# Attention's 416 steps written out with constant waits and addresses; gathers that take their indices straight from the sorted table and from src

## What is computed

```
h = relu(layernorm(x))
# layer 0: idx = both directions of the edge list
ngl, ngr = (h @ Wl.T), (h @ Wr.T)                  # 4 heads of 16
gl, gr = ngl[idx_src], ngr[idx_dst]
score  = (att * leaky_relu(gl + gr, 0.2)).sum(-1)
alpha  = softmax of score over the edges of one idx_src
out    = segment_sum(gr * alpha, idx_src)
x = x + gelu(concat([out, h]) @ W1.T + b1) @ W2.T + b2
# layer 1
h = relu(layernorm(x))
agg = segment_sum(h[src] + edge_attr, dst)
y = relu(agg @ W1 + b1) @ W2 + b2
x = x + batchnorm(y)
```

## Time and profile before

| | |
|---|---|
| median of 3 runs | 9004.02 us (8930.97 to 9032.82) |
| the profiled execution | 9012.64 us, span 9010.8 us |
| attention, from its first gather to its last | 1127.5 to about 6308 us |
| messages, first gather | 6676 us |
| granted clock of PE | 0.537 of full speed in the mean |

### The profile page before, as it was taken

One profiled execution on the slowest core, in us unless ns is written; L12 is line 12 of the kernel. 1 busy time (PEld: TensorE's weight loads), 2 busy tenths in 40 slices (PEclk: granted clock), 3 DMA queues, 4 the chain that ended last, 5 costly groups with the idle time before them and its releaser, 6 DMA issues. The chain is left out here.

```text
span 9010.8 us, 65938 instructions
## 1 busy us (share of the span) xinstructions
PE 2933.2 (33%) x13731; PEld 2480.9 (28%) x13731; DVE 5072.6 (56%) x7913; ACT 1027.4 (11%) x1576; POOL 5385.2 (60%) x4913
## 2 busy tenths in 40 slices
PE   1011122533544333354444334343341112121223
PEld 1011122423434333353333334343220111111112
DVE  9999922745756565575656556564832323333334
ACT  3001100101111111011111101010210101001101
POOL 0000066767777776777777776777036666667774
PEclk9975555555555555555555555555555555555555
DMA  1000022323433333343333333337311111111211
GB/s 30 0 0 0 9 73 65 104 74 85 107 92 93 90 87 85 83 109 91 86 90 88 87 87 91 87 95 71 69 38 44 47 45 48 44 46 46 48 44 31
DMA packets 530967, 588.05 MB, mean 65 GB/s; under 512 B 274126, under 2 KB 277326, under 8 KB 530466
## 3 DMA queue, kind: packets, MB, share of 16 engines
q1 hardware_dynamic: 370066, 421.03, 15.4%
q0 software_dynamic: 156672, 160.75, 11.6%
q10 hardware_dynamic: 3984, 3.89, 0.2%
HBM read 467.65 MB, written 117.55 MB: 65 GB/s over the span
## 5 line engine op out<-in xcount | busy, mean ns | idle before, releaser
L827 POOL DMA_INDIRECT rows<-gr_table,stage x3328 | 3799.1, 1142 | 2345.4 <-DVE stage L1009 1319.7
L882 PE MATMUL bank<-gl_step,hot_t 128*128 128x64 f32 x6720 | 1562.6, 412 | 2205.7 <-issue 1395.0
L882 PEld LDWEIGHTS bank<-gl_step,hot_t 128*128 128x128 f32 x6720 | 1503.1, 327 | 2335.4 <-issue 1660.5
L1337 POOL DMA_INDIRECT message<-h_table,edge_stage x1568 | 1565.3, 998 | 781.8 <-issue 663.3
L1030 DVE TENSOR_TENSOR fore<-bank,rows 128x512 f32<-128x512 f32 x416 | 283.7, 682 | 1472.0 <-remote 803.5
L1358 PE MATMUL bank<-edge_parts,edge_hot 128*128 128x192 bf16 x1568 | 286.4, 363 | 1789.1 <-DVE edge_parts L1428 1201.5
L889 PE MATMUL bank<-parts,hot_sum 128*128 128x204 bf16 x3328 | 681.5, 374 | 484.0 <-issue 403.1
L1358 PEld LDWEIGHTS bank<-edge_parts,edge_hot 128*128 128x128 bf16 x1568 | 202.7, 140 | 1872.7 <-DVE edge_parts L1428 1259.7
L889 PEld LDWEIGHTS bank<-parts,hot_sum 128*128 128x128 bf16 x3328 | 508.3, 159 | 587.1 <-issue 451.0
L967 ACT CAST parts<-terms 128x544 bf16<-128x544 f32 x416 | 268.5, 645 | 2978.7 <-DVE terms L1038 1804.0
L1053 DVE TENSOR_TENSOR hot_sum<-iota_row,place 128x1024 bf16<-128x1024 f32 x416 | 504.5, 1213 | 6.8 <-issue 6.7
(11 more groups left out here) (267 smaller groups left out, 4355.4 us busy)
## 6 DMA issues: line engine op xcount, KB each, us to landing
place_b<-place_rows SPq DMA_DIRECT2D x422, 256.0 KB
gr_rows<-rows SPq DMA_DIRECT2D x416, 256.0 KB
rows_again<-gr_rows SPq DMA_DIRECT2D x416, 256.0 KB
rows<-gr_table,stage POOLq DMA_INDIRECT x3328
edge<-in_edge_attr SPq DMA_DIRECT2D x97, 512.0 KB
gl_step<-gl_table SPq DMA_DIRECT2D x844, 32.0 KB
message<-h_table,edge_stage POOLq DMA_INDIRECT x1568
pen_s<-pen_rows ACTq DMA_DIRECT2D x56, 64.0 KB
```

Source lines behind the costliest of these rows:

```text
L827: pool.indirect_dma_start(rows[k][:, g, :], None, m.gr_table[:, :], bass.IndirectOffsetOnAxis(stage[k][:, g:g + 1], 0)).then_inc(s_gath[k] ...
L882: last = pe.matmul(bank[slot % LAG][:, g * D:(g + 1) * D], hot_t[slot % LAG][:, g * P:(g + 1) * P], gl_s[slot][:, g // GROUP_TILES, :], st ...
L1337: pool.indirect_dma_start(rows[k][:, e, :], None, m.h2_table[:, :], bass.IndirectOffsetOnAxis(stage[k][:, e:e + 1], 0)).then_inc(s_gath[k] ...
```

## The change

In both stages the index copies are gone, with their tiles, their semaphore and POOL's wait for it. A gather now reads its 128 indices from one column of `row_of` or of `src_sb`. In attention all loops with a register are written out, so that all waits and addresses are constants. The last chunk also no longer loads the penalties of a chunk that is not there (four DMAs on ACT's queue).

The diff, cut to its core:

```diff
+    def loop(part, body):
+        for i in range(outer):
+            body(part, part.c * outer + i, i == 0)
-        body(part, part.c * outer, True)
-        with eng.Fori(part.c * outer + 1, part.c * outer + outer) as j:
-            body(part, j, False)
...
+        for c in range(CHUNKS + 1):
             turn(Part(c))
-        with eng.Fori(2, CHUNKS) as c:
-            turn(Part(c))
-        turn(Part(CHUNKS))
...
                     at_least(pool, s_store[k], j * 16)
                     at_least(pool, s_z, q - U + 1)
-                    pool.wait_ge(s_staged, q + 1)
                     pool.sem_inc(s_pool, 1)
                     for g in range(STEP_TILES):
+                        tile = q * STEP_TILES + g
                         pool.indirect_dma_start(rows[k][:, g, :], None, m.gr_table[:, :],
-                                                bass.IndirectOffsetOnAxis(stage[k][:, g:g + 1], 0)).then_inc(s_gath[k], 16)
+                                                bass.IndirectOffsetOnAxis(m.row_of[:, tile:tile + 1], 0)
+                                                ).then_inc(s_gath[k], 16)
...
                     if part.score:
                         dve.wait_ge(s_leaky, q + 1)
                         dve.tensor_tensor(weighed[:, :, :], leaky[:, :, :], att, ALU.mult).then_inc(s_weighed, 1)
-
-                        at_least(dve, s_gath[(k - 1) % U], (j + (k > 0)) * 16 * STEP_TILES)
-                        stage_of((k - 1) % U, q + U - 1).then_inc(s_staged, 1)
                     if part.sum:
                         dve.wait_ge(s_mid, r + 1)
...
                 at_least(pool, s_message, h - U + 1)
-                pool.wait_ge(s_staged, h + 1)
                 pool.sem_inc(s_pool, 1)
                 for e in range(HALF):
+                    tile = h * HALF + e
                     pool.indirect_dma_start(rows[k][:, e, :], None, m.h2_table[:, :],
-                                            bass.IndirectOffsetOnAxis(stage[k][:, e:e + 1], 0)).then_inc(s_gath[k], 16)
+                                            bass.IndirectOffsetOnAxis(m.src[:, tile:tile + 1], 0)).then_inc(s_gath[k], 16)
...
-                    if h + U - 1 < HALVES:
-                        at_least(dve, s_gath[(h - 1) % U], ((h - 1) // U + 1) * 16 * HALF)
-                        stage_of((h - 1) % U, h + U - 1).then_inc(s_staged, 1)
                     dve.wait_ge(s_edge[g % V], (g // V + 1) * 16)
                     dve.wait_ge(s_gath[k], (h // U + 1) * 16 * HALF)
```

More of the change, by code:

```diff
@@ L102, in __init__ @@
     def __init__(self, eng, sem):
-        self.eng, self.sem, self.n, self.turns = eng, sem, 0, 0
+        self.eng, self.sem, self.n = eng, sem, 0
     def link(self, ins):
@@ L107, in link @@
         ins.then_inc(self.sem, 1)
-        self.eng.wait_ge(self.sem, self.turns + self.n)
+        self.eng.wait_ge(self.sem, self.n)
 class Memory:
@@ L749, in attention @@
     factor = sb("factor", [P, HEADS], F32, ctx)
-    s_staged = sem("s_staged")
     s_pool = m.s_pool
@@ L786, in __init__, with walk @@
         def __init__(self, c):
-            known = isinstance(c, int)
             self.c = c
-            self.score = not known or c < CHUNKS
-            self.sum = not known or c >= 1
-    def loop(eng, part, body):
-        body(part, part.c * outer, True)
-        with eng.Fori(part.c * outer + 1, part.c * outer + outer) as j:
-            body(part, j, False)
-    def walk(eng, turn):
-        for c in range(2):
+            self.score = c < CHUNKS
+            self.sum = c >= 1
+    def loop(part, body):
+        for i in range(outer):
+            body(part, part.c * outer + i, i == 0)
+    def walk(turn):
+        for c in range(CHUNKS + 1):
             turn(Part(c))
-        with eng.Fori(2, CHUNKS) as c:
-            turn(Part(c))
-        turn(Part(CHUNKS))
     def sums_of(slot, i):
@@ L865, in turn @@
             def turn(part):
-                loop(sp, part, body)
+                loop(part, body)
                 if part.score:
@@ L940, in turn @@
             def turn(part):
-                loop(pe, part, body)
+                loop(part, body)
                 if part.score:
                     scan(part)
-            walk(pe, turn)
+            walk(turn)
         def half_of_weights(i):
@@ L973, in turn @@
                 if part.sum:
-                    loop(act, part, body)
+                    loop(part, body)
                 if not part.score:
@@ L1023, in body @@
                     tile = q * STEP_TILES - part.c * CHUNK_TILES
-                    if not isinstance(tile, int):
-                        tile = nc.s_assert_within(tile, 0, CHUNK_TILES - STEP_TILES, skip_runtime_bounds_check_because=
-                                                  "a chunk's steps are its tiles")
                     dve.wait_ge(s_step, q + 1)
@@ L1135, in scan @@
                 dve.wait_ge(s_weights_act, c + 1)
-            for k in range(U - 1):
-                stage_of(k, k).then_inc(s_staged, 1)
             chain.link(dve.memset(m.acc[:, :, :, :], 0.0))
@@ L1149, in turn @@
                 c = part.c
-                loop(dve, part, body)
+                loop(part, body)
                 if part.sum:
@@ L1157, in turn @@
                 if part.score:
-                    before = chain.n
-                    if not isinstance(c, int):
-                        chain.turns = (c - 2) * SCAN_LINKS
                     scan(part)
-                    if part.sum:
-                        assert chain.n - before == SCAN_LINKS, chain.n - before
-            walk(dve, turn)
+            walk(turn)
 def attention_nodes(m, ctx):
@@ L1305, in messages @@
     edge = [sb(f"edge{k}", [P, 2, HALF, D], F32, ctx) for k in range(V)]
-    stage = [sb(f"edge_stage{k}", [P, HALF], I32, ctx) for k in range(U)]
     hot = [sb(f"edge_hot{k}", [P, HALF, P], BF16, ctx) for k in range(4)]
```

20 lines of the change are left out of this document (6 added, 14 removed).

## The result

Over 20 executions of each the changed kernel takes 8917.51 us in the median (8842.46 to 8987.9) and the kernel before 8971.78 (8910.76 to 9059.44). The ratio is 0.9936, with a 95% interval of 0.9913 to 0.9959: about 54 us less.

What follows compares the result with a forecast made beforehand. POOL's chain of gathers was taken to bound attention, and less strictly messages. +130 - 107 - 75 = -52 against the profiled 9012.6 us gives 8961, or 8955 us in terms of the median; range 8750 to 9110.

Steps and rivals of the forecast that it cites:

- The same holds less strictly: Messages: as in attention, POOL's chain of gathers sets the length, with 195 us of stops.
- The door, +130: Attention: without the index copy 268 gathers get in 0.64 us later, at L136; 0.76 of 172 us, bounds 0 and +172.
- Stops in attention, -107: Attention: POOL may go one step further; -72 at chunk ends, -30 mid-chunk, -5 in chunk 0; bounds 0 and -356.
- All of these stretches end with POOL's stop: Attention, 13 mid-chunk stops: slow PE stretches last until POOL stops, so one extra step makes them 10 us longer; -30 us.
- the 0 us for the written-out loops: Attention: dropping register instructions and jumps gains nothing on POOL; on DVE, PE, ACT and SP they lie in waits for rows.
- 14.4 was forecast: Attention, chunk ends: POOL resumes 4.4 us earlier and has an extra step of 10.0 us, at each of five stops; -72 us.
- Messages, -75: Messages: one half of 10 us more before each of 25 stops; taken between -23 and -185 us.
- the stops come 10 us further apart: Messages, case where POOL's stop releases DVE: the stops only come later each time; -23 us.
- they vanish: Messages, case where DVE's wait has a length of its own: all stops under 10 us go; -185 us.
- The door is needed: Attention, against the rival that gathers get in between L1056 and L1062 without the copy: 8825 us, chance 0.18.
- the stops in messages did not vanish: Against the rival that the stops in messages vanish: 8845 us, chance 0.13; together with the door not needed 8715, 0.06.
- the written-out stream: Attention, rival: long code costs POOL 0.125 us of idle time for each gather, 415 us more; 9370 us, chance 0.10.

Runs made afterwards that it cites:

- the small instruction: The changed kernel with one DVE copy of 128x8 numbers into an unread tile put between L1041 and L1044: 8493.03 us, 1.0069 of the kernel before.
- the one that differs from it by a wait that never held: The changed kernel with POOL waiting for z of step q-7 in place of q-8 before gathering step q: 8623.3 us, 1.0237 of the kernel before.
- ten slots: The changed kernel with the reduction moved ahead of L1044, and in messages ten slots for gathered rows in place of six: 8838.6 us, 0.9841 of the kernel before.

## Why the prediction was right, and where it was right by luck

**The number.** 8955 us was forecast against a median of 9004, a change of -0.54%; measured is -0.64%. The time lies in the range. (From the terms as they stand the median is 9004 - 52 = 8952 us; 8955 is 3 us off.) The sum holds by luck: measured against the terms of +130, -107 and -75 are +151, -260 and +15, errors of +21, -153 and +90 that nearly cancel. The bounds of the sum did not cover this either, since they put the stops of attention at -107 although the term's own bound was -356.

**What bounds the kernel.** Right for attention: the 5084 us are 3947 of gathers, 1011 of ordinary idle time and 126 of stops. Wrong for messages. "The same holds less strictly" missed that POOL's stops there are set by the other side's rate.

**The door, +130.** Measured +151 over four traces (+116 to +178). The mechanism is shown three times: gathers of 2.98 us in place of 2.37, the small instruction that takes 135 us off, and the moved reduction that takes 127 off. The 0.64 us for each gather came out as 0.61. But the +151 are not all at the place that the term priced. By the DVE instruction at which the long gathers got in, about 110 us lie at L1038, L1041, L1044 and L136 (in the first trace 227 gathers at L136 and 140 at L1041, where 268 and 84 got in at L1009 and L1056). About 40 lie elsewhere, 28 of them at the one-hot tile L997 and 14 at L1023, which the term left out. By the rule of the Trainium skill ("SBUF — State Buffer", Who interferes with whom) the term was +172; the measured +151 lies halfway between the two.

**Stops in attention, -107.** Measured -260. Two sentences failed. The first is "All of these stretches end with POOL's stop, and so I take it that they will still end so": about 26 of the 32 that came still contain a stop, but in chunks 1 to 12 only 2 to 6 came in place of 13. The second is the 0 us for the written-out loops. I put the register instructions of DVE, PE, ACT and SP under time in which these engines wait for rows. By the table of the four kernels on one chip writing out was worth 246 us once the copies were gone. In the loops 203 of DVE's and 1085 of SP's instructions took 0.70 us; that these make up the 246 us is not shown. Here is how one of the few in the changed kernel still ends (its timeline, PE, DVE and POOL):

```profile
3970.62 0.33 PE L881 MATMUL bank<-parts,hot_sum 128*128 128x204 bf16 x1 [2.47 <-issue]
3972.02 0.33 PE L881 MATMUL bank<-parts,hot_sum 128*128 128x204 bf16 x1 [1.07 <-issue]
...
3976.31 0.37 DVE L1005 TENSOR_TENSOR acc<-acc,bank 128x204 f32 x1 [46.51 <-remote]
...
4005.99 1.39 POOL L819 DMA_INDIRECT rows<-gr_table,row_of  x1 [40.80 <-issue]
```

POOL stopped at 4005.99 - 40.80 = 3965.19, and PE was quick again from 3972 on, 7 us later. Here the scan began only then, so the stop is one of 41 us.

At chunk ends at which PE's matmuls are not slow the step was right. POOL resumed 0.78 us after L1015's end, as forecast. From the last z of the chunk to the first of the next there were 88.1 us at one such end of the kernel before and 88.2 us at one of the changed kernel; the stop was 22.2 us in the first and 5.0 in the second, 17 us less where 14.4 was forecast. Such an end is itself slow, though in another way than by PE's matmuls. Ahead of the stop of 7.50 us above, DVE does nothing for 24.68 us between two of its additions (timeline of the changed kernel, DVE):

```profile
1926.30 0.37 DVE L1005 TENSOR_TENSOR acc<-acc,bank 128x204 f32 x1 [0.39 <-issue]
1951.35 0.37 DVE L1005 TENSOR_TENSOR acc<-acc,bank 128x204 f32 x1 [24.68 <-issue]
```

How often such gaps come was not counted, and their cause stays open. The time from the last z to the first is shorter too. After chunk 0 it is 54 us and more in 19 of 22 cases of the kernel before (45.6 at the least), and 39 to 40 in 26 of 44 of the changed kernel; in the changed kernel a stop at the end of chunk 1 or a later one follows only times of 84 us and more, or (two, of 3.6 and 12.8 us) a slow stretch just ahead. On the quiet chip it is 43 us with loops and 39 without.

**Messages, -75.** Measured +15, which two traces of before (2231.0 and 2231.5) and four of the changed kernel (2240 to 2256) bear out. The step that failed is that a stop that comes later is a stop saved. It was weighed between "the stops come 10 us further apart" and "they vanish"; the third case, that the waiting side is slower in the mean and takes back whatever it is given, was not among the cases.

**The rivals.** The door is needed, the stops in messages did not vanish, and the written-out stream costs no idle time between gathers: 0.305 us in every trace. That it costs nothing at all is not shown: on the quiet chip writing out alone took 50 us more. "What would upset all of it is a change in how often PE goes slow" is what happened; that it upset the terms and not the sum is the luck above.

**The sign depends on the place.** Where the stretches do not come up there is no stop to win. The changed kernel was not run there, but the one that differs from it by a wait that never held was: 1.0237, slower by 2.4%. With the door put back it is 1.0069. That the changed kernel itself is slower there is an inference from these two. What makes a place quiet stays open.

## What to carry to other kernels

An instruction that looks like overhead can be the gap through which another engine gets to memory: before taking it out, look at who starts or ends at its row, and if it has to go, put another instruction that lets the other engine in (here the reduction, with no instruction added) into its place. A deeper queue pays only where the producer is the slower side in the mean; look at how full the queue is over the whole stage, not only at its stops. Don't price register instructions and loops at nothing before you have looked at their lengths in the trace; here some take 0.70 us in place of 0.04 to 0.06, and writing out was worth 246 us beside gathers without copies where I had put 0 (how much of it is theirs is not shown).

The best of these kernels is the changed one with the reduction moved ahead of L1044: 0.982 of the kernel before, where the changed one has 0.993 beside it. In the second comparison, with ten slots as well, it is 0.984 against 0.987, 46 us, and the two intervals overlap.

## What was not expected of the hardware

Some chips have stretches of 20 to 160 us in which many of SP's instructions take 0.70 us and PE's matmuls begin a multiple of 0.70 us apart, and in kernels with loops some of DVE's register instructions take 0.70 us too, while POOL's gathers keep to 0.95 us. In the two traces of the kernel before all 36 contain a stop of POOL and end within 11 us of the beginning of the last one; in the four of the changed kernel about 26 of 32 contain one, so some end without it. The whole kernel takes 8432.6 us on a chip without them and 8962 to 9084 on chips with them, 6% and more. No engine's busy time shows such a difference: the kernel written out with copies took 8482.78 and 9028.85 us, and in its two traces POOL is busy for 5466.1 and 5382.6 us, DVE for 5099.2 and 5056.3, PE for 2885.7 and 2908.7. What begins the stretches, and whether it is POOL's stop that ends them, is not settled.
